# Opening of an attention kernel: mask rows written by VectorE instead of transfers, constants over two queues, batch 0 loaded alone, weights prepared in a later step

## What is computed

```python
qkv = x @ W_qkv + b_qkv                        # on the layer norm of x; 16 query heads, 4 key/value heads, width 8
scores = jnp.einsum('bkgsd,bktd->bkgst', q, k) / np.sqrt(HEAD_DIM)
scores = jnp.where(causal, scores, -jnp.inf)
attn = jax.nn.softmax(scores, axis=-1)
y = jnp.einsum('bkgst,bktd->bkgsd', attn, v)   # then y @ W_out + b_out
...
delta = THRESH_FACTOR * jnp.mean(jnp.abs(w))
w_eff = jnp.where(w > delta, 1.0, jnp.where(w < -delta, -1.0, 0.0)) * alpha
...
x = x + _layernorm(_L0_attn_ref(_layernorm(x), ...))
x = x + _layernorm(_L0_ffn_ref(_layernorm(x), ...))
```

## Time and profile before

| | |
|---|---|
| median of 3 runs | 492.5 us (489.48 to 495.44) |
| the profiled execution: time, span | 494.3 us, 492.5 us |
| mean granted TensorE clock | 0.968 |
| busy: TensorE, VectorE, ScalarE, GpSimd | 85%, 79%, 66%, 60% of the span |
| first `mx` product starts | 47.85 us |

### The profile page before, as it was taken

One profiled execution on the slowest core, in us unless ns is written; L12 is line 12 of the kernel. 1 busy time (PEld: TensorE's weight loads), 2 busy tenths in 40 slices (PEclk: granted clock), 3 DMA queues, 4 the chain that ended last, 5 costly groups with the idle time before them and its releaser, 6 DMA issues.

```text
span 492.5 us, 18291 instructions
## 1 busy us (share of the span) xinstructions
PE 419.3 (85%) x6918; PEld 291.4 (59%) x6918; DVE 389.9 (79%) x1299; ACT 323.5 (66%) x577; POOL 294.7 (60%) x551
## 2 busy tenths in 40 slices
PE   0321899989999999999999999998999999999641
PEld 0211666666667676767677757775677677665330
DVE  1310878889999999999899989997999998995532
ACT  0220147667778787888888878886788788768521
POOL 0140223356777777777777767775777776756663
PEclk9999999999999999999999999998999999999855
DMA  5757334333632363335333533354333433331121
GB/s 145 170 113 91 52 56 97 77 76 76 116 77 73 79 159 75 75 75 150 76 77 75 148 82 76 77 134 87 68 75 71 120 78 76 75 89 29 28 63 43
DMA packets 77587, 42.85 MB, mean 87 GB/s; under 512 B 13084, under 2 KB 73276, under 8 KB 77500
## 3 DMA queue, kind: packets, MB, share of 16 engines
q1 hardware_dynamic: 77500, 41.68, 38.4%
HBM read 13.85 MB, written 4.72 MB: 38 GB/s over the span
## 4 chain that ended last, share of the span: by engine, by line
PE 57%; DVE 9%; DMA 8%; POOL 7%; issue 7%; SPq 7%; ACT 3%; POOLq 0%; DVEq 0%; ACTq 0%
PE ps_y L802 13%; PE ps_mx L828 12%; PE ps_st L781 11%; PE ps_w L854 6%; DMA den<-Y 4%; DVE M L632 4%; PE ps_w L882 4%; PE ps_w L891 3%; POOL yn L425 3%; PE ps_w L892 2%; SPq L279 2%; PE ps_w L874 2%; DVE stats L590 2%; PE ps_w L841 2%; PE ps_w L864 2%
## 5 line engine op out<-in xcount | busy, mean ns | idle before, releaser
L632 DVE TENSOR_REDUCE M<-ps_mx 128x2 f32<-128x512 f32 (+3 forms) x448 | 219.3, 530 | 42.0 <-PE ps_mx L828 40.2
L457 ACT ACTIVATE PT<-ps_st 128x1024 f32<-128x1024 f32 (+1 forms) x192 | 168.6, 881 | 25.7 <-PE ps_st L781 15.2
L828 PE MATMUL ps_mx<-KS,QS 112*64 112x64 bf16 (+2 forms) x2560 | 133.8, 229 | 23.1 <-DMA KS<-part 19.3
L828 PEld LDWEIGHTS ps_mx<-KS,QS 112*64 112x64 bf16 x2560 | 90.9, 114 | 69.1 <-issue 27.4
L781 PE MATMUL ps_st<-QS,KS 114*64 114x256 bf16 (+1 forms) x1024 | 104.9, 306 | 0.0
L802 PE MATMUL ps_y<-PT,VB 128*32 128x256 f32 (+3 forms) x2048 | 103.8, 309 | 0.9 <-ACT PT L457 0.9
L397 POOL TENSOR_TENSOR rstd<-vareps,mhalf 128x2 f32<-128x2 f32 x128 | 88.9, 694 | 10.0
L432 POOL TENSOR_TENSOR rest<-QK,part 128x512 f32<-128x512 f32 x32 | 37.1, 1160 | 43.2 <-ACT part L486 43.2
L395 POOL TENSOR_TENSOR vareps<-mv,eps 128x2 f32<-128x2 f32 x128 | 25.7, 201 | 54.7 <-DVE mv L602 54.5
L500 ACT CAST MpT<-ps_w 16x512 bf16<-16x512 f32 x32 | 18.4, 575 | 56.3 <-PE ps_w L864 56.3
L781 PEld LDWEIGHTS ps_st<-QS,KS 114*64 114x64 bf16 x1024 | 47.7, 110 | 13.0 <-issue 2.2
(11 more groups left out here) (59 smaller groups left out, 507.6 us busy)
## 6 DMA issues: line engine op xcount, KB each, us to landing
QS<-part SPq DMA_DIRECT2D x192, 64.0 KB
rden<-rec_dram SPq DMA_DIRECT2D x32, 256.0 KB
X<-in_x SPq DMA_DIRECT2D x8, 512.0 KB, 6.3
out<-X SPq DMA_DIRECT2D x8, 512.0 KB, 5.0
KS<-part SPq DMA_DIRECT2D x32, 96.0 KB
QS<-qfb SPq DMA_DIRECT2D x4, 512.0 KB
KS<-part SPq DMA_DIRECT2D x32, 64.0 KB
KS<-kfb SPq DMA_DIRECT2D x4, 264.0 KB
```

Of the source, the lines that this page charges most:

```text
L457: nc.scalar.activation(PT[n % 2][:, 0:512 * banks], ps_st[n % 2][:, 0:banks, :].rearrange("p a c -> p (a c)"), ACT.Exp, scale=SCALE).then_ ...
L632: last = nc.vector.tensor_reduce(m[:, pair:pair + pairs, i], ps_mx[n % 2][:, at:at + w].rearrange("p (h t) -> p h t", h=pairs), AX_X, ALU.max)
L828: last = pe.matmul(ps_mx[n % 2][64 * one:64 * one + 64, at:at + w], q[:, h, BL * i:BL * i + BL], k[:, kv, blocks, :], start=True, stop=Tru ...
```

## The change

The mask rows move from rows 48 to 111 to rows 0 to 63 of `QS` and `KS`, and the parts from rows 0 to 47 to rows 64 to 111 (`r = BL + HD * c`). The mask constants come as 64 rows. VectorE writes the mask rows with two copies for each of the four buffers (`fill`), and `mx` of the first four batches waits for the copies of its buffer (`s_fill`). The two rows of -1 come from a tile that GpSimd sets, by four small transfers on ScalarE's queue. The load of the first group is cut into batch 0 (on `s_x0`) and batches 1 to 3. The constants are spread over the queues of SyncE and ScalarE and over five semaphores, and each engine waits for those it needs. The ternary weight and the bias are prepared in `constants()` and `ternary()`, after VectorE's steps 1 and 2 and after TensorE's step 2, through `ps_y` in place of `ps_w`. TensorE waits for their results ahead of step 5 (ATT). All steps from 3 on have the same instructions in the same order as before.

```diff
         @block.sync
-            load(0)
-            for dst, src in consts:
-                sp.dma_start(dst[:], src).then_inc(s_const, 16)
-
-            sp.wait_ge(s_fix, 2)
-            for i in range(RING):
-                sp.dma_start(QS[i][PARTS:MAXROW], qfb[PARTS:MAXROW, :].unsqueeze(1)
-                             .broadcast_to([BL, NH, S])).then_inc(s_fixed, 16)
-                sp.dma_start(KS[i][PARTS:ROWS], kfb[PARTS:ROWS, :].unsqueeze(1)
-                             .broadcast_to([ROWS - PARTS, NKV, KLEN])).then_inc(s_fixed, 16)
-
-            sp.wait_ge(s_setg, 1)
-
-            sp.wait_ge(s_fixed, FIXED)
+            sp.dma_start(X[:, 0:TT, :], xv[0, :, 0:TT, :]).then_inc(s_x0, 16)
+            sp.dma_start(wq_sb[:], wq).then_inc(s_early, 16)
+            for dst, src in ((qf_sb, qfix), (kf_sb, kfix)):
+                sp.dma_start(dst[:], src).then_inc(s_mconst, 16)
+            sp.dma_start(X[:, TT:GRP * TT, :], xv[0, :, TT:GRP * TT, :]).then_inc(s_x, 16)
+            for dst, src in ((wf_sb, wf), (al_sb, alpha), (bf_sb, bf)):
+                sp.dma_start(dst[:], src).then_inc(s_late, 16)
...
-                    sp.dma_start(QS[i][HD * c:HD * c + HD, :, :], src[:, 0, :]).then_inc(s_stack[i], 16)
+                    r = BL + HD * c
+                    sp.dma_start(QS[i][r:r + HD, :, :], src[:, 0, :]).then_inc(s_stack[i], 16)
...
         @block.scalar
-            act.wait_ge(s_const, CONST)
+            for dst, src in ((id_sb, ident), (wk_sb, wk), (bq_sb, bq), (bk_sb, bk)):
+                act.dma_start(dst[:], src).then_inc(s_early, 16)
+            for dst, src in ((wv_sb, wv), (vm_sb, vmask)):
+                act.dma_start(dst[:], src).then_inc(s_vconst, 16)
+            for dst, src in ((wo_sb, wo), (bv_sb, bvw), (bo_sb, bo)):
+                act.dma_start(dst[:], src).then_inc(s_late, 16)
+            act.wait_ge(s_setg, 1)
+            for i in range(RING):
+                act.dma_start(KS[i][MAXROW:ROWS], neg[:].unsqueeze(1).broadcast_to([2, NKV, KLEN])).then_inc(s_neg, 16)
+
+            act.wait_ge(s_early, EARLY)
             run_steps(step)
...
         @block.vector
+            def fill(i):
+
+                dve.wait_ge(s_cast, 2)
+                nc.vector.tensor_copy(QS[i][0:BL], qfb[:].unsqueeze(1).broadcast_to([BL, NH, S])).then_inc(s_fill, 1)
+                nc.vector.tensor_copy(KS[i][0:BL], kfb[:].unsqueeze(1).broadcast_to([BL, NKV, KLEN])).then_inc(s_fill, 1)
+
+            def masks():
+                dve.wait_ge(s_mconst, MCONST)
+                nc.vector.tensor_copy(qfb[:], qf_sb[:]).then_inc(s_cast, 1)
+                nc.vector.tensor_copy(kfb[:], kf_sb[:]).then_inc(s_cast, 1)
...
-            run_steps(step)
+            step(Step(0))
+            masks()
+            fill(0)
+            step(Step(1))
+            fill(1)
+            constants()
+            step(Step(2))
+            fill(2)
+            fill(3)
+            ternary()
+            for t in range(3, STEPS):
+                step(Step(t))
 
         @block.tensor
...
+                    if b < RING:
+                        pe.wait_ge(s_fill, 2 * b + 2)
...
-            run_steps(step)
+            pe.wait_ge(s_early, EARLY)
+            for t in range(3):
+                step(Step(t))
+            constants()
+            for t in range(3, ATT):
+                step(Step(t))
+            pe.wait_ge(s_weff, 1)
+            pe.wait_ge(s_bo, 1)
+            for t in range(ATT, STEPS):
+                step(Step(t))
```

More of the change, by code:

```diff
@@ L110, in build @@
         idb = sb("idb", [128, 128], BF16)
[L111 to L114, removed]
+        qf_sb = sb("qf_sb", [BL, S], F32)
+        kf_sb = sb("kf_sb", [BL, KLEN], F32)
+        qfb = sb("qfb", [BL, S], BF16)
+        kfb = sb("kfb", [BL, KLEN], BF16)
+        neg = sb("neg", [2, KLEN], BF16)
         vm_sb = sb("vm_sb", [128, 2 * NLO * NB, HD], F32)
@@ L164, in build @@
         ps_w = psum("ps_w", [128, 512])
-        s_const = sem("s_const")
+        s_early = sem("s_early")
+        s_vconst = sem("s_vconst")
+        s_mconst = sem("s_mconst")
+        s_late = sem("s_late")
+        s_neg = sem("s_neg")
+        s_x0 = sem("s_x0")
         s_x = sem("s_x")
@@ L170, in build @@
         s_setg = sem("s_setg")
-        s_fix = sem("s_fix")
-        s_fixed = sem("s_fixed")
+        s_cast = sem("s_cast")
+        s_fill = sem("s_fill")
         s_bo = sem("s_bo")
@@ L216, in build @@
         s_fin = sem("s_fin")
[L218 to L221, removed]
+        EARLY, VCONST, MCONST, LATE, NEG = 16 * 5, 16 * 2, 16 * 2, 16 * 6, 16 * RING
         STACK = 16 * 9
-        FIXED = 16 * 2 * RING
         WORK = {"v": (SPLIT, s_vb), "op": (OUT, s_a1), "turn": (TURN, s_mt), "x1": (PROJ, s_xt), "ff": (FFN, s_f1),
@@ L549, in _ @@
             dve.memset(ones[:], 1.0).then_inc(s_wchain, 1)
[L550 to L571, removed]
@@ new lines, in constants @@
+            def constants():
+                dve.wait_ge(s_early, EARLY)
+                nc.vector.tensor_copy(idb[:], id_sb[:]).then_inc(s_setup, 1)
+                dve.wait_ge(s_vconst, VCONST)
+                for i in range(RING):
+                    last = nc.vector.tensor_copy(VB[i][:, :, HD:2 * HD], vm_sb[:])
+                last.then_inc(s_setup, 1)
+                dve.wait_ge(s_late, LATE)
+                nc.vector.tensor_scalar(wneg[:], wf_sb[:], -1.0, None, ALU.mult).then_inc(s_wchain, 1)
+                dve.wait_ge(s_wchain, 2)
+                nc.vector.tensor_tensor(wabs[:], wf_sb[:], wneg[:], ALU.max).then_inc(s_wchain, 1)
+                dve.wait_ge(s_wchain, 3)
+                nc.vector.reduce_sum(wsum[:], wabs[:], AX_X).then_inc(s_setup, 1)
@@ new lines, in ternary @@
+            def ternary():
+                dve.wait_ge(s_wps, 1)
+                for j in range(TT):
+                    last = nc.vector.tensor_tensor(bo_sb[:, j, :], ps_y[:, 1, 0:D], bo_sb[:, j, :], ALU.add)
+                last.then_inc(s_bo, 1)
+                nc.vector.tensor_scalar(delta[:, 0:1], ps_y[:, 0, 0:1], 1.0 / (D * D), 0.7, ALU.mult,
+                                        ALU.mult).then_inc(s_wchain, 1)
+                dve.wait_ge(s_wchain, 4)
+                nc.vector.tensor_scalar(delta[:, 1:2], delta[:, 0:1], -1.0, None, ALU.mult).then_inc(s_wchain, 1)
+                dve.wait_ge(s_wchain, 5)
+                nc.vector.tensor_scalar(wabs[:], wf_sb[:], delta[:, 0:1], None, ALU.is_gt).then_inc(s_wchain, 1)
+                nc.vector.tensor_scalar(wneg[:], wf_sb[:], delta[:, 1:2], None, ALU.is_lt).then_inc(s_wchain, 1)
+                dve.wait_ge(s_wchain, 7)
+                nc.vector.tensor_tensor(wneg[:], wabs[:], wneg[:], ALU.subtract).then_inc(s_wchain, 1)
+                dve.wait_ge(s_wchain, 8)
+                nc.vector.tensor_scalar(weff[:], wneg[:], al_sb[:, 0:1], None, ALU.mult).then_inc(s_weff, 1)
+                dve.wait_ge(s_bo, 1)
```

49 lines of the change are left out of this document (22 added, 27 removed).

## The result

| | before | changed |
|---|---|---|
| median, beside each other | 493.97 us (489.48 to 496.70, 4 runs) | 468.26 us (467.76 to 468.68, 4 runs) |
| ratio, 95% interval | | 0.949 (0.944 to 0.954) |
| the same again, other runs | 492.05 us (7 runs) | 469.52 us (467.48 to 472.12, 4 runs), 0.955 (0.950 to 0.960) |
| the profiled execution: time, span | 494.3 us, 492.5 us | 467.8 us, 465.9 us |
| first `mx` product | 47.85 us | 25.80 us |

A forecast was written before the change was run, and what follows sets the result against it. Bound taken: batch 0's parts wait behind mask transfers, after constants and weight preparation; later steps are pipeline-bound. Step 3 moving from 47.85 to 23.2 us saves 24.6, from median 492.5 to 468 us; forecast's own range 465 to 471, 8-in-10 range 462 to 476.

The forecast's parts named there:

- Batch 0's first part: Opening, from batch 0's load through layer norm and ScalarE's issues and copy: first part ready at 12.8 us.
- Batch 0's transfers: Nine part transfers before step 3: last landing between 20.5 and 25.9 us, the middle, 23.2, taken.
- The row of batch 2: Earlier trace: part at 56.65 us, DMA engines quiet by about 65.7, read as 9.0 us of transfers, giving 21.8.
- VectorE: VectorE's work before its first maxima, with four fills at 1.8 us: through at 23.1, allowing step 3 at 22.4.
- The rival of slow fills: VectorE's mask copies cost per element and set step 3's start: 473 or 485 us; chance 0.13.
- The lock between the two engines: VectorE and GpSimd in the opening: a fill meeting a GpSimd operation costs up to 1.2 us, time 468.4.
- What is moved without a price: Waits for `weff` and `bo_sb` moved to step 5, -1 rows and `s_fill` waits: no added cost.
- The sum: Step 3 starts at the later of 23.2 and 22.4 us, 24.6 us earlier than 47.85; median 468 us.
- The same 445 us behind step 3: Steps 3 to 41 keep their 445 us; a change of more than 2 us would mean being wrong.
- slow transfers: Batch 0's parts take 13.1 us, ScalarE is late, step 4 waits 1 or 2 us: 472 to 473 us; chance 0.12.
- The slower steps: Parts landing in rows 64 to 111 slow each of 32 steps; at 1 us a step, 500 us; chance 0.03.
- Start without end: Step 3 starts earlier but the pipeline behind doesn't end as much earlier: 475 to 485 us; chance 0.06.

The follow-up runs named there:

- run 1: Changed kernel with the mask rows written by eight transfers on SyncE's queue instead of VectorE's copies: 480.21 us, first `mx` at 37.76.
- run 2: Kernel before with VectorE writing the mask rows, the rows exchanged and -1 rows by four transfers: 479.48 us against 493.38, ratio 0.971.
- run 3: Changed kernel with the weight preparation put back ahead of step 0, on VectorE and TensorE: 477.48 us, first `mx` at 33.04.
- Run 6: Changed kernel with only the four transfers of -1 rows moved from ScalarE's queue to SyncE's: 468.01 us, first `mx` at 23.23.
- run 10: Changed kernel with batch 1's part transfers held back until batch 0's nine have landed: 468.93 us, first `mx` at 24.74.
- run 4: Changed kernel with all constants and -1 rows on SyncE's queue, ScalarE issuing nothing: 469.20 us, first `mx` 1.95 us earlier.
- run 5: Changed kernel run again unchanged, for its time and a second profile: 469.52 us, first `mx` at 26.0.
- run 9: Kernel before with only mask rows and part rows exchanged, all still by transfers: 491.37 us against 491.62, ratio 0.999.
- run 11: Changed kernel with -1 rows on SyncE's queue and ScalarE's table load made early by a small exponential: 467.06 us, first `mx` at 22.1.
- run 12: Changed kernel with -1 rows on SyncE's queue, early table load and idle TensorE products (16 and 8): 466.69 us, ratio to before 0.950.
- run 8: Changed kernel with idle TensorE products, 16 ahead of step 0 and 20 ahead of the first `mx`: 467.63 us.

## Why the prediction was right, and where not

**What bounded the kernel** was read rightly. Runs 1 and 2 price the mask transfers at 12.0 and 12.35 us of start, taken out of the changed kernel and put into the one before; run 3 prices the place of the weight preparation at 7.2. The last 2.5 us are a remainder.

**Batch 0's first part** was due at 12.8 and came at 13.95. The layer norm was exact (5.9 forecast, 6.04 measured), and so was the choice of ScalarE as the later one. The term that was mis-sized is the four transfers of -1 rows: 0.6 us each by the small issues of the earlier trace rows, 3.26 for the four in the trace, with the first at 1.27; they also began 0.2 us later. Run 6 gives that back and more.

**Batch 0's transfers** were put at 10.4 us (23.2 - 12.8) and took 11.8. The 10.4 was the middle between 13.1 us, which was sound, and 7.7, the spread of the issues and 2.0 us of landing. That 2.0 is the term that was mis-sized: the last transfer took 5.93 us from its issue to its landing, and 4.9 (19.84 to 24.7) in run 10 with nothing behind it. The row of batch 2, which was to speak for short transfers, misled in the same way: I took the end of the traffic for the landing. Run 10 shows 1.7 us between the two; with as much (an estimate) batch 2's 9.0 us become 10.7, next to the 10.8 that batch 0's nine took alone. These two terms, 1.15 and 1.4 us, are the 2.6 us by which the first `mx` was late (25.80 against 23.2).

**VectorE** was due at 23.1 and was through at 24.1. It lost that microsecond at batch 2's layer norm, which waited 2.58 us for GpSimd behind batch 0's third part: fill 2 was due at 17.6 and began at 18.61. The fills were right to a few per cent: 1.75 us a pair from start to start, against 1.8 by the price per byte. From the two copies, 0.54 us for 2048 elements is 0.26 ns an element. The Trainium skill, "Vector Engine (DVE) Microarchitecture Reference", section 5.1, has four elements a cycle for this form. The estimate from it in the prediction, 1.6 us for the 6144 elements of a pair, is 0.26 ns an element, and the trace agrees. The rival of slow fills is refuted. The lock between the two engines was of the right kind, but the wrong one was to pay: a fill was to wait up to 1.2 us. Fills 2 and 3 took what the others took (1.21 and 0.68 us), and GpSimd waited: batch 1's subtraction took 3.27 us in place of 1.16, because two pairs of copies stood back to back. It cost nothing, since batch 1's parts are not late for step 4. A fill that waited is seen in run 4, 0.95 us.

**What is moved without a price** held: no wait of TensorE on `weff`, `bo_sb` or the -1 rows appears behind the first `mx`.

**The sum** was 24.6 us of start; 22.05 were measured. That the time came out at 468.26 against 468 is luck to some 2 us: the start was 2.6 us late, and executions with a short stretch behind it made that good. The second comparison, 22.5 us, is what the start explains. "The same 445 us behind step 3" was true of the second profile (444.3) and not of the first (440.1), which is past the 2 us that the prediction itself set as a sign of being wrong. The prediction had no term for when TensorE reaches its higher speed, which by run 5 is worth some 3.7 us there.

**The rivals**: slow transfers were partly true (11.8 of 13.1, and ScalarE 1.2 late), without the delay of step 4. The slower steps are refuted by run 9. Start without end didn't happen for the 22 us of the change. Below that it is open: runs 4, 6, 11 and 12 start step 3 another 1.95 to 3.7 us sooner, and their medians are 0.9 us above to 2.8 us below the changed kernel's.

## What to carry to other kernels

In an opening, look for data that stands finished while a queue is busy with something else; a copy by an engine that is idle there anyway (1.75 us) can replace transfers that hold a queue for 4 us a pair. Before spreading transfers over an engine's queue, count their issues against that engine's own first work: here 13 of them made ScalarE the late one, and one queue did as well as two. And count a transfer to its landing, not to the end of its traffic. Last, an opening that is 2 us shorter needs more than four executions to be told, when the executions of one kernel differ by 4.

## What the runs showed that I had not expected

- VectorE's copies, back to back, can keep a GpSimd operation out for the whole row of them: 3.27 us for an operation of 1.16 that met fills 2 and 3, 10.22 when four pairs more stood between those. The Trainium skill, "SBUF — State Buffer", section "Who interferes with whom", gives the lock to whichever issues first for its whole instruction; the rows agree that it is exclusive. But in these rows GpSimd got no turn between two copies, and in run 4, where its subtraction began 0.11 us after a copy, it did. What decides between the two is not shown.
- 1.7 us go by between the last traffic of a batch's parts and their landing (run 10).
- Four transfers of 8 KB onto two partitions took 3.26 us to issue on ScalarE's queue and 2.9 on SyncE's, more than four of 64 KB or 128 KB constants at 0.47 each.
- One and the same kernel reaches TensorE's higher speed about 8 us after its first `mx` in one execution and 25 to 27 after in another. Up to step 5 that is worth 3.7 us, as much as the whole gain of run 11's opening. Idle products bring the higher speed from the first `mx` on, but in runs 8 and 12 the granted clock then fell to half for 6.8 and 3.4 us near 42 us, as it did for 3.4 us in the changed kernel's first profile.
